# Small masked score units share a bank between heads, and the query groups run 0 1 2 3 4 6 7 5 with the first and the last in halves

## What is computed

```python
q_in = rope(x); q, k = q_in @ Wq.T + bq, q_in @ Wk.T + bk; v = x @ Wv.T + bv
scores = einsum('bqhd,bkhd->bhqk', q, k) * scale
scores = where(tril(ones((S, S))), scores, -inf)          # causal
ctx = einsum('bhqk,bkhd->bqhd', softmax(scores), v)
x1 = layer_norm(x + ctx @ Wo.T + bo)
gates = softmax(x1 @ gate_w.T + gate_b); top2 = top_k(gates, 2)
moe = sum(gate[e] * (x1 @ expert_w[e].T + expert_b[e]) for e in top2)
x = layer_norm(x + layer_norm(x1 + moe))
```

## Time and profile before

| | us |
|---|---|
| median of 3 runs | 1549.48 (1547.62 to 1550.94) |
| the profiled execution | 1549.67 |
| its span, first to last instruction | 1547.9 |
| TensorE busy | 1455.6 (94%) |
| VectorE busy | 1090.7 (70%) |
| ScalarE busy | 814.5 (53%) |
| GpSimd busy | 425.7 (28%) |
| mean granted TensorE clock | 0.974 |

### The profile page before, as it was taken

One profiled execution on the slowest core, in us unless ns is written; L12 is line 12 of the kernel. 1 busy time (PEld: TensorE's weight loads), 2 busy tenths in 40 slices (PEclk: granted clock), 3 DMA queues, 4 the chain that ended last, 5 costly groups with the idle time before them and its releaser, 6 DMA issues.

```text
span 1547.9 us, 27399 instructions
## 1 busy us (share of the span) xinstructions
PE 1455.6 (94%) x9264; PEld 764.6 (49%) x9264; DVE 1090.7 (70%) x2736; ACT 814.5 (53%) x1899; POOL 425.7 (28%) x704
## 2 busy tenths in 40 slices
PE   8889999999999999999999999998999979999677
PEld 6667755565444464453656554444443333343242
DVE  3667667678777887877755677777778877887135
ACT  3235345555556556646565546453665637556631
POOL 4335544232322231221424332322111101110114
PEclk9999999999999999999999999998999989999888
DMA  4745432124010230010217131113000000010000
GB/s 119 197 136 135 112 87 54 50 66 109 23 46 26 53 98 15 24 38 23 64 31 168 47 92 31 49 46 86 19 23 15 23 15 15 22 26 19 22 1 14
DMA packets 143369, 86.60 MB, mean 56 GB/s; under 512 B 106430, under 2 KB 136390, under 8 KB 142975
## 3 DMA queue, kind: packets, MB, share of 16 engines
q1 hardware_dynamic: 143231, 84.85, 21.4%
HBM read 58.76 MB, written 25.43 MB: 54 GB/s over the span
## 4 chain that ended last, share of the span: by engine, by line
PE 55%; DVE 5%; ACT 3%; issue 3%; POOL 1%; SPq 1%; DMA 1%; POOLq 0%; DVEq 0%; ACTq 0%
PE bank L1307 12%; PE bank L1418 11%; PE bank L1287 11%; PE bank L1261 9%; ACT pbuf L913 2%; DVE mxs L998 2%; PE bank L1377 1%; PE bank L1396 1%; SPq L741 1%; PE bank L1265 1%; DMA qs<-eb_nmT 1%; PE bank L1290 1%; PE bank L1413 1%; PE bank L1338 1%; PE bank L1344 1%
## 5 line engine op out<-in xcount | busy, mean ns | idle before, releaser
L998 DVE TENSOR_REDUCE mxs<-bank 128x1 f32<-128x512 f32 (+3 forms) x1280 | 729.6, 603 | 190.9 <-PE bank L1265 122.2
L913 ACT ACTIVATE pbuf<-bank 128x512 f32<-128x512 f32 (+3 forms) x1312 | 609.7, 533 | 337.7 <-PE bank L1307 173.9
L1287 PE MATMUL bank<-qs,ks 99*128 99x512 bf16 (+3 forms) x1312 | 446.6, 350 | 22.2 <-DMA qs<-eb_nmT 18.4
L1261 PE MATMUL bank<-ks,qs 96*128 96x512 bf16 (+3 forms) x1280 | 442.4, 353 | 4.8 <-DVE mxs L998 3.4
L1307 PE MATMUL bank<-pbuf,vcur 128*17 128x512 f32 (+3 forms) x2624 | 266.2, 523 | 10.3 <-ACT pbuf L913 9.9
L1287 PEld LDWEIGHTS bank<-qs,ks 99*128 99x128 bf16 x1312 | 129.9, 99 | 242.9 <-issue 137.2
L1418 PE MATMUL bank<-ew,x1T 128*128 128x512 f32 x464 | 228.0, 614 | 0.0
L1261 PEld LDWEIGHTS bank<-ks,qs 96*128 96x128 bf16 x1280 | 126.5, 99 | 144.7 <-issue 42.6
L1307 PEld LDWEIGHTS bank<-pbuf,vcur 128*17 128x17 f32 x2624 | 60.5, 97 | 142.6 <-issue 106.1
L1418 PEld LDWEIGHTS bank<-ew,x1T 128*128 128x128 f32 x464 | 82.9, 194 | 66.4 <-issue 62.4
L1290 PE MATMUL bank<-idb,maskb 128*128 128x128 bf16 x512 | 111.9, 220 | 0.0
(11 more groups left out here) (263 smaller groups left out, 1715.2 us busy)
## 6 DMA issues: line engine op xcount, KB each, us to landing
parts_scratch<-parts SPq DMA_DIRECT2D x29, 384.0 KB, 3.4
vcur<-v_scratch SPq DMA_DIRECT2D x80, 136.0 KB, 2.4
xw<-windows SPq DMA_DIRECT2D x29, 256.0 KB, 3.1
qs<-parts_scratch SPq DMA_DIRECT2D x32, 192.0 KB, 3.3
ks<-parts_scratch SPq DMA_DIRECT2D x32, 192.0 KB, 3.2
ks<-parts_scratch SPq DMA_DIRECT2D x32, 128.0 KB, 2.8
qs<-parts_scratch SPq DMA_DIRECT2D x32, 128.0 KB, 3.4
v_scratch<-vst SPq DMA_DIRECT2D x29, 136.0 KB, 1.8
```

The lines of the kernel that those rows point to most:

```text
L913: nc.scalar.activation(pbuf[:, i % PB, r0:r1], bk[:, r0:r1], ACT.Exp)\
L998: v.reduce_max(mxs[:, j * HJ + h, c:c + 1], bk[:, 0:width], AX_X).then_inc(emptied[b], 1)
L1261: last = mm(bk[:, 0:width].rearrange("p (n t) -> p n t", t=P), qs5[0:KR, pos % QRING, j, head, :], ks5[0:KR, kslot, 0:width // P, head, :] ...
L1287: last = mm(bk[:, r0:r1].rearrange("p (n t) -> p n t", t=P), ks5[0:KR + NPART, kslot, kb % GT, head, :], qs5[0:KR + NPART, place(J) % QRIN ...
```

## The change

Three things. First, units of the diagonal that are small share a bank: four heads with 128 columns each, or two with 256. With four, one mask matmul of 512 columns (the mask or the identity repeated by a stride of 0) opens the bank and the four score matmuls add to it; with two, each keeps its own mask. One reduce or one exponential then reads the whole bank. The same rule holds for every score unit of a halved group, whose key tiles have 256 columns or fewer. Second, `ORDER` puts group 5 last, and it is halved as group 0 is. Third, the planner's costs of the matmuls and the ranks of the a_ and r_ steps from tile 20 on change.

```diff
-ORDER = (0, 1, 2, 3, 4, 5, 6, 7)
-HALVED = (0,)
+ORDER = (0, 1, 2, 3, 4, 6, 7, 5)
+HALVED = (0, 5)
...
+def heads_together(cols):
+
+    return HJ if cols == P else HJ // 2 if cols == 2 * P else 1
...
+@functools.lru_cache(None)
+def mx_list(J):
 
     s, hg, j0, nj = JOBS[J]
-    c, j, h = i // (nj * HJ), j0 + i // HJ % nj, i % HJ
-    return c, j, h, (j + 1) * P if c == s % GB else GQ
-
-
-def st_units(J):
-    return HJ * key_tiles(J)
-
-
-def st_before(J):
-    return sum(st_units(x) for x in range(J))
+    out = []
+    for c in range(keys_groups(J)):
+        for j in range(j0, j0 + nj):
+            cols = (j + 1) * P if c == s % GB else GQ
+            n = heads_together(cols)
+            out += [(c, j, h, n, cols) for h in range(0, HJ, n)]
+    return out
...
+def st_list(J):
+
+    out = []
+    for kb in range(key_tiles(J)):
+        lo, hi = st_tiles(J, kb)
+        n = heads_together((hi - lo) * P)
+        out += [(kb, h, n, (hi - lo) * P) for h in range(0, HJ, n)]
+    return out
+
+
+def st_last(J, kb):
+
+    return max(i for i, x in enumerate(st_list(J)) if x[0] <= kb)
...
-            turn += -5
+            turn += -5 if T < 20 else -5 - (T - 20) / 4 if T < 28 else -7
...
-            rows["mx", J, i] = ("PE", cols / 2.4 + 3 + 56 * diag, r + length * i / n,
...
+            rows["mx", J, i] = ("PE", heads * max(cols / 2.4 + 3, 98) + (220 if cols == P else 95 * heads) * diag, r + length * i / n,
                                 [(f"kst{k}", newest) for k in range(3)] +
                                 [(f"qst{k}", LATE.index(newest)) for k in range(3)])
...
-            rows["st", J, i] = ("PE", cols / 2.4 + 3 + 56 * diag, r + length * i / n,
...
+            rows["st", J, i] = ("PE", heads * max(cols / 2.4 + 3, 98) + (220 if cols == P else 95 * heads) * diag, r + length * i / n,
...
+                    nc.scalar.activation(pbuf[:, u0:u0 + heads, nj * P - cols:nj * P],
+                                         bk[:, 0:heads * cols].rearrange("p (h t) -> p h t", h=heads), ACT.Exp)\
...
+                    v.reduce_max(mxs[:, j * HJ + h:j * HJ + h + heads, c],
+                                 bk[:, 0:heads * cols].rearrange("p (h t) -> p h t", h=heads), AX_X)\
+                        .then_inc(emptied[b], 1)
...
+                    if heads == HJ:
+
+                        mm(bk[:, :].rearrange("p (h t) -> p h t", h=HJ), idb[:, :],
+                           maskb[:, :].unsqueeze(1).broadcast_to([P, HJ, P]), start=True, stop=False)
+                    for x in range(heads):
+                        head = hg * HJ + h + x
+                        last = mm(bk[:, x * cols:(x + 1) * cols].rearrange("p (n t) -> p n t", t=P),
+                                  qs5[0:KR, pos % QRING, j, head, :], ks5[0:KR, kslot, 0:cols // P, head, :],
+                                  start=heads < HJ, stop=x == HJ - 1 or not diag)
+                        if diag and heads < HJ:
+                            last = mm(bk[:, x * cols + j * P:x * cols + (j + 1) * P], idb[:, :], maskb[:, :],
+                                      start=False, stop=True)
                     last.then_inc(filled[b], 1)
                 elif name == "nm_T":
...
+                        mm(bk[:, :].rearrange("p (h t) -> p h t", h=HJ), maskb[:, :],
+                           idb[:, :].unsqueeze(1).broadcast_to([P, HJ, P]), start=True, stop=False)
...
-                        pe.wait_ge(*drain("st", J, HJ * (kb + 2) - 1))
+                        pe.wait_ge(*drain("st", J, st_last(J, kb + 1)))
```

## The result

The changed kernel takes 1492.76 us (median of 4 runs, 1491.53 to 1494.73) where the kernel before took 1548.82 on the same chip. The ratio is 0.9638, 95% interval 0.9621 to 0.9654, so 56 us less. 17 us less were forecast.

The account below looks back on a forecast made before the run. TensorE, busy for 94% of the span, was taken as the bound. The terms -1.0 + 2.9 - 5.8 - 12.1 - 0.8 = -16.8 us took 1549.67 us to 1532.9, say 1533, with a range of 1519 to 1550.

Parts of the forecast that it names:

- Both lie beside TensorE work, so 0 ... I bound it at -3 to +6.: Shared banks: VectorE and ScalarE savings hidden; longer-held banks and the planner's shifted order bounded at -3 to +6, taken as 0.
- the mask's -1.0: Small units: four 128-column mask matmuls become one of 512 in 72 units, 1.0 us less TensorE work.
- rival B: Mask matmuls: each 128-column one truly costs its 99 ns weight load, so -12.8 for -1.0, 1521 us; chance 0.05.
- Together +2.9: Group 5 in halves: 24 more key tiles add 0.5 us of scores and 2.4 of value matmuls; bounds 0.5 to 5.
- The turn 5 to 6 (10.8) goes ... -5.8.: New group order: the 10.8 us loss between groups 5 and 6 goes, 4 to 6 costs 5 (0 to 14).
- That is 7 ... in place of 19.1: -12.1: Last attention job: shorter with group 5 halved, its loss falls from 19.1 to 7 us (4 to 14).
- I take 24 (14 to 30) for 24.8: Tail behind the last job: two tiles left instead of four, loss 24 us for 24.8, so -0.8.
- the 43 to 46 that I named as a sign: Tail: a length of 43 to 46 us in the changed profile would show the forecast right.
- rival A: Tail fills better with spilled expert work: tail loss 14, last job 5, 12 us less, 1521 us; chance 0.18.
- Rival E: Eight short jobs at the end: bare DMA round trips of the maxima, 6.7 us each, make 1560 us; chance 0.15.
- Rival D: Turn into group 7: keys of tile 31 come late, half of 24 us bare, +12, 1545 us; chance 0.10.
- Rival C: Bare turn 4 to 6 (14) and last job with full round trip (14) leave some 3 us, 1548; chance 0.12.

Follow-up runs that it names:

- x5: Changed kernel with group order 0 to 7, only group 0 halved, old ranks and old prices, so bank sharing alone: 1487.8 us, ratio 0.9621.
- x7: Changed kernel with the same order, banks and matmuls, but readers of a shared bank working head by head: 1495.8 us, ratio 0.969.
- y4: x5 with six rotating banks instead of seven: 1520.8 us, ratio to the kernel before 0.9824.
- x2: Changed kernel with one head per bank and old prices; new order, halves and ranks stay: 28 us slower than the kernel before.
- x4: Changed kernel with the planner's old matmul prices; sharing, new order, halves and ranks stay: ratio 0.9693 to the kernel before.
- y3: x5 with each four-head bank opened by four 128-column masks instead of one of 512: 1490.8 us, ratio 0.9656.
- y5: x4 without the halving of group 5, so sharing with order 4, 6, 7, 5: 1501.0 us, ratio 0.9688.
- x3: Kernel before with only the planner's new matmul prices: 30 us less than the kernel before.
- x1: Changed kernel with the order, halves and ranks taken back; sharing and new prices stay: 51 us less than the kernel before.

## Why the prediction was wrong, step by step

**"Both lie beside TensorE work, so 0 ... I bound it at -3 to +6."** This is the step that failed. Sharing as a whole, this term and the mask's -1.0, measured -58 (x5), so the term put at 0 is about -55. Its first half was right in the main: readers' time is hidden (x7, 3 to 8 us). Its second half had the wrong sign. I saw a reader that waits for four heads and holds its bank longer, and didn't set against it that four turns become one. From the records, first matmul of a unit (in a shared one, the mask) to the end of its reader, a 128-column unit held a bank for 1.02 us in the maxima and 0.74 in the scores before; in x5 four heads hold it for 2.00 and 1.52, so 0.50 and 0.38 a head. In all, attention holds banks for 4181 us before and 3854 in x5. A 128-column unit gives TensorE 0.058 + 0.058 us of work for a turn that takes six to nine times as long, and wherever the turns of several such units stand close, the seven banks can run out. How a turn saved becomes 0.16 to 0.20 us on the path stays open: the bank waits fall by 31 us of the 58 and, as y4 shows, don't go with the time; 327 us of bank time spread over seven banks is 47 us, which has the size, but the banks are far from always held.

That the time fell at all as forecast is luck. The terms that were to bring the gain, order and last job, together with the halves cost 28 us by themselves (x2) and 11 on top of sharing (x4 against x5). The gain came from a term put at 0.

**Why I didn't see it.** I read the earlier trace rows and the middle stretch of the earlier trace rows as a TensorE that is nearly full: loss 1.2 us in 50. By the distance of starts the same stretch of the kernel before loses 4.6. The row that I quoted for the spacing, 0.22 us long and 0.06 us from the next start, showed that the records overlap by more than the stalls are long. I used it for the price of a mask and not for the loss. Nor did I look at the waits of weight loads at all.

**"I take -1.0"** for the masks held by the start times (1.4 from y3's rows), with 3 us more by the medians of y3; rival B, 99 ns each, is out.

**"Together +2.9"** for the halves: the usual distances add up to 0.5 us more in x4 than in x5, and the time can't be told from the unhalved one (y5). The line through two records of value matmuls took part of the drain for work. What the term left out are the bank turns: with a bank for each head, 96 more.

**"The turn 5 to 6 (10.8) goes ... -5.8."** It went, and more came: +11 to +13 with sharing (y5 against x5). The table by places shows where. In place 5 x5 loses 8.5 us with group 5, the changed kernel 19.3 with group 6; in place 6 it is 22.0 against 35.1. The worse ratio at 4 to 6 was named and priced at 5; place 5 lost 11 more than in x5. The turn 6 to 7 I had left as it was. It still takes the same 12.6 us, but the first-layer steps and fillers that stand beside place 6 in the old order are used up a place earlier in the new one. That last reason is argued only.

**"That is 7 ... in place of 19.1: -12.1"**, the last job: its direction was right and its size too small, idle and slow clock fell from 19.1 to 1.9 us, not to 7. The round trip is partly hidden as said, by expert matmuls, 0.94 us bare. In the changed kernel's order of time:

```profile
1410.81 0.38 PE L1307 MATMUL bank<-qs,ks 99*128 99x256 bf16 x2 [0.94 <-DMA qs<-eb_nmT]
1411.90 0.39 PE L1307 MATMUL bank<-qs,ks 99*128 99x256 bf16 x2
1412.12 1.88 PE L1440 MATMUL bank<-ew,x1T 128*128 128x512 f32 x4
```

But the gain is no gain against x5. There, with the old order, the exponentials' waits in a last job of 53.2 us leave TensorE 10.5 us idle instead of 15.5 and the clock stays up, as the maxima run ahead and expert work stands beside the scores:

```profile
1370.90:1424.10 53.20, 42.75 (x248) 15.85 (x247) 11.84 (x38) 34.26 (x72) 11.27 (x19) 1.00 0.07 21
1424.10:1488.20 64.10, 48.55 (x128) 24.02 (x126) 33.67 (x118) 12.17 (x36) 20.74 (x36) 0.79 0.03 9
```

**"I take 24 (14 to 30) for 24.8"**, the tail: 14.5 + 0.12 x 46.4 = 20.1. That measure counts too much in both kernels, as part of the slow clock lies where no matmul is left (the clock is the third number from the end; the second row follows the last matmul):

```profile
1432.00:1482.00 50.00, 46.40 (x130) 21.67 (x129) 29.56 (x109) 12.27 (x36) 20.25 (x34) 0.93 0.07 22
1482.00:1492.90 10.90, 0.00 (x0) 0.00 (x0) 5.55 (x15) 0.84 (x2) 5.33 (x10) 0.62 0.07 24
```

By the distance of starts the tail's loss falls from 14.8 to 8.3. The tail is 60.9 us long, not the 43 to 46 that I named as a sign, because 41 us of TensorE work are in it by usual distances (36 before): 80 expert matmuls, those of late tiles 27 to 31, where the old tail has the 64 of tiles 28 to 31. That is rival A's mechanism, expert work that spills past the last job. Rival A had 14 for the tail and 5 for the last job, 12 less than the forecast's 24 and 7; 20.1 and 1.9 are 9 less, so it came most of the way and was hidden under what the order cost elsewhere. The chain that ended last shows it full of expert matmuls at full speed, 24 in 10.5 us twice over, and then the same end of VectorE and GpSimd steps:

```profile
1453.41 0.87 PE bank L1435 x2
1454.28 10.50 PE bank L1440 x24
...
1467.43 1.72 PE bank L1440 x4
1469.15 0.62 PE bank L1435 x2
1469.77 10.51 PE bank L1440 x24
1480.28 0.03 issue
1480.31 0.49 DVE ks L1203
```

**Rival E**, bare round trips in the short jobs, did not come; the largest such wait among the short jobs at the end is the 0.94 us above. Over the whole span scores' waits for that DMA are as many us as before (18.4 there, in 14 waits):

```profile
PE bank L1307 <- DMA qs<-eb_nmT: 18.2, 19, 5.1
```

Rival D, late keys, did not show either; the turns wait for VectorE. Rival C, saved losses that come back elsewhere, is what the order by itself did, hidden under the gain from sharing.

**The prices**, costed at nothing, are worth 30 us to a kernel without sharing. x3's bank waits are as many as before (79.3 us in 242), so it isn't that. Its granted clock is 0.984 for 0.974, which is at most 16 of the 30. What it is stays open: a planner that believes small matmuls slower spreads them out, and TensorE's loss falls from 209 to 177, mostly ahead of the steps of the first layers and the experts (76 to 55 us). That is a guess; no run separates the spreading from other effects of the prices. It matters for sharing too, as the two gains overlap: 30 and 58 apart, 51 together (x1).

## What to carry to other kernels

Count the turns of a scarce buffer, not only the work of the engines around it: here each turn of a small unit that fell away, 0.1 us of TensorE work and up to 1 us of a bank, gave 0.16 to 0.20 us under the old plan and 0.06 under a better one, though every reader had time to spare. Read a full TensorE by the distance of starts, since a record's modelled drain covers every stall that is shorter. And time the parts of a change one by one: here one part gives 58 us, another costs 11 on top of it, and the sum looked like a success of both. Time the static plan as a part of its own, too.

## What the runs showed of the hardware that I had not expected

Weight loads of 99 ns don't slow a stream of 128-column matmuls: one starts every 55 to 60 ns, and 204 mask matmuls more cost 3 us by the medians (y3). An operand repeated by a stride of 0 opens a bank for four heads in one matmul of 0.22 us. Reads in a row overlap in the records, so mean durations overstate what merging them saves: VectorE was busy for 11 us less and ScalarE for 17 between x7 and the changed kernel, where sums of means had given 25 and some 45.
